# A transformer block of four samples on one core: the token shift, norm and feed-forward part of a layer done by halves of the tokens

## The chip, the cores and the metric

One core of a Trainium2 chip. The engines are PE (TensorE; PEld is its weight load), DVE (VectorE), ACT (ScalarE), POOL (GpSimd) and SP (SyncE, which here only issues DMAs). Each runs its own list of instructions in order and waits on semaphores. The metric is the device time of one execution in microseconds.

## What is computed

Four samples of 512 tokens x 128 channels, all in float32. Each goes through a first cross attention, then two layers of the kind below, then a second attention block, and a mixture of experts. Only the layer matters here:

```
def _layer(x, wqkv, qs, ksc, wo, lg, lb, w1, b1, w2, b2):
    ...                                    # local attention over windows of 64, 8 heads of 64
    x = x + o @ wo
    h = shift_token(x)                     # second half of the channels: from the token before
    mu = h.mean(-1, keepdims=True)
    var = h.var(-1, keepdims=True)
    h = (h - mu) / jnp.sqrt(var + 1e-05) * lg + lb
    h = h @ w1 + b1                        # 128 -> 2 x 341
    a, g = jnp.split(h, 2, axis=-1)
    h = a * jax.nn.gelu(g, approximate=False)
    x = x + h @ w2 + b2                    # 341 -> 128
    return x
```

## The kernel before

The 512 tokens of a sample lie as `TILES` = 4 tiles of `P` = 128 partitions. There are two slots of buffers (u = 0 and 1); slot 0 takes samples 0 and then 2, slot 1 takes 1 and then 3. For each engine a generator `sample_steps` yields once a step, and `in_turn` runs the generators of the two slots in turn after the list `TURNS`: slot 0 is ten steps ahead, and from there on one step of slot 0 alternates with one of slot 1. A third stream, `deferred_experts`, puts the experts of samples 0 and 1 between the steps of samples 2 and 3, chunk by chunk. So the order on each engine is fixed when the program is built, and step k of slot 0 stands beside step k-10 of slot 1.

A layer has 23 steps. Step 0 transposes y into `hTs`. Steps 1 to 8 project q, k and v of the four tiles (L438, L443 on PE), rotate q and k (`rotate`, L1141 and L1145 on DVE; `add_partners`, L1549 on POOL), transpose q (`turn_q`, L450) and k (`turn_k`, L457), sum squares (L1152) and compute inverse norms (`inverse_norms`, L1159 to L1164, in steps 4 and 8), by which POOL then scales k (`normalise_k`, L1555). Steps 9 and 10 make the first scores (L469 on PE, `take_scores`, L1122 on DVE). Steps 11 to 15 are the attention loop: exponentials (L855 on ACT), division (L1509 on POOL), transposes, mixing with the values (L499), output projection (L509) and, on DVE, `add_attention` (L1195), which adds tiles 0 to 3 to y in steps 13 to 16.

What stands behind that is here called the tail of the layer. In step 16 SP waits for the last tile of y and issues four DMAs that write `shifted` (L1714, L1716 twice, L1717). In step 18 DVE takes the norm's statistics (L1091, L1094), POOL computes `rstd` with an add and a power (L1491, L1492), in step 19 DVE applies it (L1100). In step 20 PE transposes the four tiles (L425) and ACT copies them with gain and bias (L840). In step 21 PE expands (three chunks, each a gate product, L705, into one of the 3 `act_psum` banks and a value product, L708, into one of the 4 `dve_psum` banks), ACT applies Gelu (L1012), DVE adds the bias and multiplies (L1378). In step 22 PE contracts (L715) and DVE adds the residual (L1383), which POOL had made in step 17 (L1495). There are 8 tails, counted here in order of time by the start of their shift: tail 1 (sample 0, layer 0) at 96.6 us, tail 2 (sample 1, layer 0) at 147.0, tail 3 at 203.0, tail 4 (sample 1, layer 1) at 254.5, tail 5 at 482.7, tail 6 at 543.2, tail 7 at 609.7 and tail 8 at 670.0 us; 5 to 8 are those of samples 2 and 3. Steps 17 to 19 hold nothing for PE and ACT.

ACT must have the table of the function it applies: Exp, Gelu and the experts' Silu need different ones, and the compiler puts a load of 1283 ns where the function changes (in the rows of the chain an entry `ACT L...` without a tile's name is such a load). A wait on a semaphore stands on an engine's list like an instruction, so all that is behind it waits too.

## Time and profile before

| | |
|---|---|
| time, median of 3 | 886.76 us (885.13 to 886.98) |
| the profiled execution | 885.65 us, of which its span 883.9 us |
| busy: PE, DVE, ACT, POOL | 82%, 64%, 60%, 34% of the span |
| granted TensorE clock | 0.902 of 2.4 GHz on average |
| table loads on ACT | 56, of 1283 ns each |

A row of the timeline gives the start in us, the duration, engine and line, the output and inputs, and in brackets how long the engine stood idle before it and what ended that. The chain of work that ended last is followed back from the last instruction; its rows give the start, the time on the chain and the work. The rows that are used stand below the change.

### The profile page before, as it was taken

Reading aid. Unit: us, or ns where it says so; the run is one execution under the profiler, and the core shown is the slowest. Engines: PE = TensorE matmul, PEld = TensorE weight load, DVE = VectorE, ACT = ScalarE, POOL = GpSimd, SP = SyncE. Lnnn points to the kernel's source line nnn. Section 1 sums busy time; section 2 is a strip of 40 time slices with the busy share of each in tenths; the row PEclk is TensorE's granted clock in tenths of the full one; section 3 lists DMA queues with packets and bytes.
Section 4 is the critical chain, followed back from the end, with each engine's and each line's share of the span. In section 5 each row is a group of like instructions: output and inputs, shape, how many; then the busy total and the mean of one; then the engine's idle time right before and its main releaser. Section 6 shows DMA issues by size and latency. Waiting matters only on the chain.

```text
span 883.9 us, 15786 instructions
## 1 busy us (share of the span) xinstructions
PE 723.4 (82%) x5368; PEld 472.7 (53%) x5368; DVE 569.2 (64%) x2212; ACT 533.9 (60%) x1345; POOL 304.5 (34%) x296
## 2 busy tenths in 40 slices
PE   5758788897878775788869789869887898889997
PEld 3436465564556654554546465546564664675443
DVE  5676856778657748648867757647566575873623
ACT  3348495775827336355596695795785845544442
POOL 4254524455421233223445324335233124312200
PEclk9888999998987978789999999999899898879999
DMA  8610010101100000202121301200202001004252
GB/s 260 193 29 15 14 43 13 39 6 22 34 13 1 2 1 1 82 2 68 36 67 37 90 14 45 75 1 22 69 26 56 18 26 30 13 13 125 73 129 91
DMA packets 37162, 41.83 MB, mean 47 GB/s; under 512 B 14345, under 2 KB 23771, under 8 KB 36955
## 3 DMA queue, kind: packets, MB, share of 16 engines
q1 hardware_dynamic: 37083, 40.83, 16.8%
q8 instruction: 43, 0.70, 0.3%
q14 instruction: 36, 0.29, 0.1%
HBM read 28.75 MB, written 2.62 MB: 35 GB/s over the span
## 4 chain that ended last, share of the span: by engine, by line
PE 45%; DVE 26%; ACT 17%; POOL 6%; issue 3%; DMA 1%; SPq 1%; DVEq 0%; POOLq 0%; ACTq 0%
ACT work L855 8%; PE act_psum L606 5%; PE moe_psum L616 5%; PE dve_psum L438 4%; PE act_psum L499 3%; PE dve_psum L509 3%; DVE work L1122 3%; DVE stats L1091 2%; DVE res_nrm L1100 2%; PE act_psum L705 2%; PE act_psum L768 2%; PE dve_psum L708 2%; PE dve_psum L715 2%; POOL work L1509 2%; PE act_psum L425 2%
## 5 line engine op out<-in xcount | busy, mean ns | idle before, releaser
L1509 POOL TENSOR_TENSOR work<-work,rinv 128x512 f32<-128x512 f32 (+1 forms) x72 | 77.6, 1085 | 147.2 <-DVE rinv L1108 146.8
L855 ACT ACTIVATE work<-work,nbias,rnorm 128x128 f32<-128x128 f32 x256 | 122.6, 481 | 7.9 <-DVE nbias L1185 7.5
L1491 POOL TENSOR_SCALAR rstd<-mv 128x4 f32<-128x4 f32 x36 | 10.0, 277 | 173.0 <-DVE mv L1094 172.8
L1549 POOL TENSOR_TENSOR hT<-hT,work 128x512 f32<-128x512 f32 x32 | 40.7, 1271 | 77.9 <-DVE work L1145 77.9
L438 PE MATMUL dve_psum<-wqkv,hTs 128*128 128x512 f32 x128 | 66.0, 640 | 1.5 <-ACT hTs L1002 1.3
L838 ACT COPY v_loc<-act_psum 77x512 f32<-77x512 f32 (+2 forms) x72 | 41.5, 582 | 36.0 <-PE act_psum L443 16.6
L1122 DVE CUSTOM_DVE_ANT_0 work<-dve_psum,masks 128x128 f32<-128x128 f32 x256 | 58.3, 282 | 3.3 <-PE dve_psum L469 3.3
L425 PE MATMUL act_psum<-ident,res_nrm 128*128 128x128 f32 x96 | 25.3, 363 | 41.9 <-DVE res_nrm L1100 41.9
L838 ACT COPY hT<-act_psum 128x512 f32<-128x512 f32 (+1 forms) x60 | 31.1, 523 | 43.7 <-PE act_psum L499 22.4
L953 ACT ACTIVATE work<-act_psum,cols 128x512 f32<-128x512 f32 x40 | 27.4, 687 | 36.3 <-PE act_psum L606 36.2
L1555 POOL TENSOR_TENSOR v_loc<-v_loc,rnorm 128x512 f32<-128x512 f32 x32 | 33.3, 1062 | 46.0 <-DVE rnorm L1164 46.0
L1141 DVE TENSOR_TENSOR hT<-dve_psum,tab_a 128x512 f32<-128x512 f32 x32 | 22.1, 690 | 41.8 <-PE act_psum L450 25.6
L1108 DVE RECIPROCAL rinv<-sums 128x4 f32<-128x4 f32 x96 | 14.4, 167 | 52.5 <-ACT work L855 52.5
L855 ACT ACTIVATION_READ_ACCUMULATOR work<-work,nbias,rnorm 128x1 f32 x256 | 48.0, 188 | 0.0
L840 ACT ACTIVATE hT<-act_psum,cols 128x512 f32<-128x512 f32 x16 | 12.4, 775 | 54.9 <-PE act_psum L425 54.9
L425 PEld LDWEIGHTS act_psum<-ident,res_nrm 128*128 128x128 f32 x96 | 14.9, 162 | 55.0 <-issue 34.7
L1145 DVE TENSOR_TENSOR work<-dve_psum,tab_b 128x512 f32<-128x512 f32 x64 | 43.6, 681 | 0.0
L1549 POOL TENSOR_TENSOR v_loc<-v_loc,work 128x512 f32<-128x512 f32 x32 | 42.0, 1313 | 0.4 <-DVE work L1145 0.4
L479 PE MATMUL dve_psum<-ident,work 128*128 128x128 f32 x128 | 21.0, 289 | 25.7 <-POOL work L1509 22.3
L469 PE MATMUL dve_psum<-kT,qT 64*64 64x128 f32 x1024 | 40.9, 306 | 0.8 <-ACT units L969 0.4
L1492 POOL TENSOR_TENSOR rstd<-rstd,neg_half 128x4 f32<-128x4 f32 x36 | 38.4, 1065 | 3.0
L855 ACT ACTIVATE work<-work,nbias 128x154 f32<-128x154 f32 x64 | 26.2, 410 | 21.3 <-DVE nbias L1238 21.3
(224 smaller groups left out, 2015.3 us busy)
## 6 DMA issues: line engine op xcount, KB each, us to landing
ahead<-cwT_dram SPq DMA_DIRECT2D x128, 64.0 KB, 2.0
v_loc<-v_loc SPq DMA_DIRECT2D x24, 256.0 KB, 3.7
kT<-cwT_dram SPq DMA_DIRECT2D x80, 64.0 KB, 2.1
qT<-cwT_dram SPq DMA_DIRECT2D x48, 64.0 KB, 2.0
wqkv<-in_wqkv_dram SPq DMA_DIRECT2D x2, 768.0 KB
res_nrm<-in_x_dram SPq DMA_DIRECT2D x4, 256.0 KB, 3.1
w_m<-in_w_m_dram SPq DMA_DIRECT2D x1, 1024.0 KB, 8.7
v_loc<-v_loc SPq DMA_DIRECT2D x8, 128.0 KB, 3.2
```

The lines of the kernel that those rows point to most:

```text
L425: last = nc.tensor.transpose(bank[:, t * P:(t + 1) * P], src[u][:, t, :], ident[:])
L438: nc.tensor.matmul(bank[:], h, attn_w[:, k * INNER:(k + 1) * INNER], start=True, stop=True)\
L469: last = nc.tensor.matmul(banks[odd][half * WINDOW:(half + 1) * WINDOW, c * KEYS:(c + 1) * KEYS], qT[u][d, c, at:at + WINDOW], kT[u][d, c, ...
L606: nc.tensor.matmul(bank[:], w, given[:], start=True, stop=True).then_inc(act_filled, 1)
L616: nc.tensor.matmul(moe_psum[:], w, units_of, start=(c == 0), stop=False)
L838: nc.scalar.copy(dst, bank[0:n, 0:w]).then_inc(act_emptied, 1)
L855: last = nc.scalar.activation(weights[:, i, :], weights[:, i, :], ACT.Exp, bias=nbias[u][:, b, i:i + 1], scale=scale_of(i), accum_out=sums ...
L1122: return nc.vector.tensor_tensor_reduce(out=weights, in0=bank[:, at:at + width], in1=mask, scale=1.0, scalar=LOWEST, op0=ALU.add, op1=ALU. ...
L1145: nc.vector.tensor_tensor(partners[u][:, t % 2, k, :].rearrange(halves, s=2, d=DH // 2), bank[:].rearrange(halves, s=2, d=DH // 2)[:, :, : ...
L1492: nc.gpsimd.tensor_tensor(rstd[u][:], rstd[u][:], neg_half[:, 0:TILES], ALU.pow).then_inc(ln_rstd[u], 1)
L1509: nc.gpsimd.tensor_tensor(some, some, by.unsqueeze(2).to_broadcast(list(some.shape)), ALU.mult).then_inc(ready[u], 1)
L1549: nc.gpsimd.tensor_tensor(own, own, partners[u][:, t % 2, k, :], ALU.add).then_inc(turned_ready[u], 1)
```

## The change

The tail is done in two halves of two tiles each. The token shift of tiles 0 and 1 is issued in step 14, as soon as `add_attention` has added tile 1; its statistics are taken in step 15, `rstd` by POOL in step 15, and it is applied in step 16. PE transposes that half in step 17, expands it in step 18 and contracts it in step 19; the second half follows the old places: shift in step 16, statistics in 18, applied in 19, transposed in 20, expanded in 21, contracted in 22. The number of steps is the same. `shifted` has two places, one for each half, and two semaphores. Gelu, the product with the gate, the copy behind the transposes and the residual add are each split into two of 256 columns, and so are the two products of the expansion; the transposes and the contraction's matmuls are as many as before. The four shift DMAs become two sets of four, each half as large, and the `rstd` pair on POOL is issued twice on half as many elements. ACT has 68 table loads where it had 56. Line numbers of the changed kernel are higher by 8 (PE, L425 to L509 there L433 to L517), 21 (ACT) and 30 to 35 (DVE).

```diff
-LN_XATTN, LN_OUTER, LN_FF, LN_TGT, LN_1, LN_2, LN_3, LN_MOE = 0, 1, (2, 3), 4, 5, 6, 7, 8
+LN_XATTN, LN_OUTER, LN_FF, LN_TGT, LN_1, LN_2, LN_3, LN_MOE = 0, 1, ((2, 3), (4, 5)), 6, 7, 8, 9, 10
+PAIR = TILES // 2
+HALVES = ((0, PAIR), (PAIR, TILES))
...
-shifted = [v[:, 2 * TILES - 1, :].rearrange("p (t d) -> p t d", t=TILES) for v in v_loc]
+shifted = [[v[:, tile, 0:PAIR * D].rearrange("p (t d) -> p t d", t=PAIR) for tile in (TILES + 1, 2 * TILES - 1)] for v in v_loc]
...
                 yield from local_attention_steps(l, u)
-                yield
-                yield
-                yield
-                transpose_norm(("hT_ff", l, u), LN_FF[l], u)
-                yield
-                pe.wait_ge(act_emptied, act_item["hT_ff", l, u] + 1)
-                for m, w in enumerate(HID_W):
-                    bank = act_bank(("ff_g", l, m, u))
-                    nc.tensor.matmul(bank[0:w, :], w1[:, l, HID + m * P:HID + m * P + w], hT[u][:],
-                                     start=True, stop=True).then_inc(act_filled, 1)
-                    bank = dve_bank(("ff_a", l, m, u))
-                    nc.tensor.matmul(bank[0:w, :], w1[:, l, m * P:m * P + w], hT[u][:],
-                                     start=True, stop=True).then_inc(dve_filled, 1)
-                yield
-                pe.wait_ge(dve_emptied, dve_item["ff_a", l, len(HID_W) - 1, u] + 1)
-                bank = dve_bank(("ff_out", l, u))
-                for t in range(TILES):
+                def turn_half(g):
+                    transpose_tiles(("hT_ff", l, u, g), nrm, u, LN_FF[l][g], *HALVES[g])
...
+                def expand_half(g):
+                    tokens = slice(HALVES[g][0] * P, HALVES[g][1] * P)
+                    pe.wait_ge(act_emptied, act_item["hT_ff", l, u, g] + 1)
...
+                def contract_half(g):
+                    pe.wait_ge(dve_emptied, dve_item["ff_a", l, len(HID_W) - 1, u, g] + 1)
+                    bank = dve_bank(("ff_out", l, u, g))
...
+                    last.then_inc(dve_filled, 1)
+
+                turn_half(0)
+                yield
+                expand_half(0)
+                yield
+                contract_half(0)
+                yield
+                turn_half(1)
+                yield
+                expand_half(1)
+                yield
+                contract_half(1)
                 yield
...
                 yield from local_attention_steps(l, u)
-                yield
-                yield
-                yield
-                copy_bank(("hT_ff", l, u), hT[u][:], bias=col("ln_b", l), scale=col("ln_g", l))
-                yield
-                for m, w in enumerate(HID_W):
-                    bank = filled(("ff_g", l, m, u))
-                    nc.scalar.activation(gel[u][0:w, m, :], bank[0:w, :], ACT.Gelu, bias=col("b1g", 3 * l + m, w))\
-                      .then_inc(act_emptied, 1)
-                yield
-                yield
+                for g in range(2):
+                    tokens = slice(HALVES[g][0] * P, HALVES[g][1] * P)
+                    copy_bank(("hT_ff", l, u, g), hT[u][:, tokens], bias=col("ln_b", l), scale=col("ln_g", l), w=PAIR * P)
+                    yield
+                    for m, w in enumerate(HID_W):
+                        bank = filled(("ff_g", l, m, u, g))
+                        nc.scalar.activation(gel[u][0:w, m, tokens], bank[0:w, 0:PAIR * P], ACT.Gelu, bias=col("b1g", 3 * l + m, w))\
+                          .then_inc(act_emptied, 1)
+                    yield
+                    yield
...
+        def shifted_stats(l, u, g):
+            dve.wait_ge((shift_early, shift_late)[g][u], 4 * 16 * (l + 1))
+            for i, t in enumerate(range(*HALVES[g])):
...
+        def shifted_apply(l, u, g):
+            dve.wait_ge(ln_rstd[u], LN_FF[l][g] + 1)
+            for i, t in enumerate(range(*HALVES[g])):
...
@@ -1215,13 +1250,17 @@
                     take_pt_lo(n, u)
                 if n >= 2:
                     add_attention(n - 2, u)
+                if n == PAIR + 1:
+                    link(nc.vector.memset(shifted[u][0][0:1, 0, D // 2:D], 0.0))
+                if n == TILES:
+                    shifted_stats(l, u, 0)
                 if n + 1 < TILES:
                     invert_sums(u, sm_local(l, n + 1), (n + 1) % 2)
                 if n + 2 < TILES:
                     take_scores(n + 2, u)
                 yield
             add_attention(TILES - 1, u)
-            link(nc.vector.memset(shifted[u][0:1, 0, D // 2:D], 0.0))
+            shifted_apply(l, u, 0)
...
                 yield from local_attention_steps(l, u)
-                yield
-                dve.wait_ge(shift_done[u], 4 * 16 * (l + 1))
-                norm_stats(shifted, u)
-                yield
-                norm_apply(LN_FF[l], shifted, nrm, u)
-                yield
-                yield
-                for m, w in enumerate(HID_W):
-                    bank = filled(("ff_a", l, m, u))
...
-                bank = filled(("ff_out", l, u))
-                dve.wait_ge(res_ready[u], l + 1)
-                nc.vector.tensor_tensor(flat(y[u]), bank[:], flat(res[u]), ALU.add).then_inc(dve_emptied, 1)
+                def gate_half(g):
+                    tokens = slice(HALVES[g][0] * P, HALVES[g][1] * P)
...
+                def add_half(g):
+                    bank = filled(("ff_out", l, u, g))
...
+                                            ALU.add).then_inc(dve_emptied, 1)
+
+                yield
+                shifted_stats(l, u, 1)
+                gate_half(0)
+                yield
+                shifted_apply(l, u, 1)
+                add_half(0)
+                yield
+                yield
+                gate_half(1)
+                yield
+                add_half(1)
                 if l == LAYERS - 1:
...
                 yield
+                norm_rstd(LN_FF[l][0], u, *HALVES[0])
                 yield
                 yield
...
                 yield
-                norm_rstd(LN_FF[l], u)
+                norm_rstd(LN_FF[l][1], u, *HALVES[1])
                 yield
...
-                for _ in range(1 + TILES + 1):
+                def shift_half(g, done):
+
+                    first, end = HALVES[g]
+                    sp.wait_ge(dve_emptied, dve_item["attn_out", l, end - 1, u] + 1)
+                    for lo, hi in ((0, 112), (112, P - 1)):
+                        sp.dma_start(shifted[u][g][lo + 1:hi + 1, :, half:D], y[u][lo:hi, first:end, half:D]).then_inc(done[u], 16)
+                    start = max(first, 1)
+                    sp.dma_start(shifted[u][g][0:1, start - first:, half:D], y[u][P - 1:P, start - 1:end - 1, half:D]).then_inc(done[u], 16)
+                    sp.dma_start(shifted[u][g][:, :, 0:half], y[u][:, first:end, 0:half]).then_inc(done[u], 16)
+
+                for _ in range(1 + PAIR + 1):
                     yield
-                sp.wait_ge(dve_emptied, dve_item["attn_out", l, TILES - 1, u] + 1)
-                sp.dma_start(shifted[u][:, :, 0:half], y[u][:, :, 0:half]).then_inc(shift_done[u], 16)
-                for lo, hi in ((0, 112), (112, P - 1)):
-                    sp.dma_start(shifted[u][lo + 1:hi + 1, :, half:D], y[u][lo:hi, :, half:D]).then_inc(shift_done[u], 16)
-                sp.dma_start(shifted[u][0:1, 1:TILES, half:D], y[u][P - 1:P, 0:TILES - 1, half:D])\
-                  .then_inc(shift_done[u], 16)
+                shift_half(0, shift_early)
+                yield
+                yield
+                shift_half(1, shift_late)
                 yield
```

On PE in tail 1, behind the output projection of tile 3 (dve_psum3 <- wo). Of before:

```order
L509 MATMUL dve_psum3<-wo,hT0 128x128 x4
L443 MATMUL act_psum0<-wqkv,hTs1 128x512
L457 MATMUL act_psum1<-ident,v_loc1 128x128 x4
L438 MATMUL dve_psum0<-wqkv,hTs1 128x512
L438 MATMUL dve_psum1<-wqkv,hTs1 128x512
L450 MATMUL act_psum2<-ident,hT1 128x128 x4
L457 MATMUL act_psum0<-ident,v_loc1 128x128 x4
L443 MATMUL act_psum1<-wqkv,hTs1 128x512
```

and of after:

```order
L517 MATMUL dve_psum3<-wo,hT0 128x128 x4
L451 MATMUL act_psum0<-wqkv,hTs1 128x512
L465 MATMUL act_psum1<-ident,v_loc1 128x128 x4
L433 MATMUL act_psum2<-ident,res_nrm0 128x128 x2
L446 MATMUL dve_psum0<-wqkv,hTs1 128x512
L446 MATMUL dve_psum1<-wqkv,hTs1 128x512
L458 MATMUL act_psum0<-ident,hT1 128x128 x4
L465 MATMUL act_psum1<-ident,v_loc1 128x128 x4
L713 MATMUL act_psum2<-hT0,w1 128x256
L716 MATMUL dve_psum2<-hT0,w1 128x256
...
L451 MATMUL act_psum2<-wqkv,hTs1 128x512
L724 MATMUL dve_psum1<-w2,qT0 128x128 x6
```

The first half's transposes now stand ahead of slot 1's q and k projection (L446), and its expansion and contraction behind that.

On DVE in the same place, from the add of tile 2 on (y0 <- dve_psum0). Of before:

```order
L1195 TENSOR_TENSOR y0<-dve_psum0,y0 128x128
L1141 TENSOR_TENSOR hT1<-dve_psum1,tab_a 128x512
...
L1195 TENSOR_TENSOR y0<-dve_psum3,y0 128x128
L1224 MEMSET v_loc0 1x64
L1152 TENSOR_REDUCE sumsq1<-res_nrm1 128x16
L1141 TENSOR_TENSOR hT1<-dve_psum0,tab_a 128x512
...
L1091 BN_STATS stats0<-v_loc0 128x6 x4
L1094 BN_AGGR mv0<-stats0 128x2 x4
L1152 TENSOR_REDUCE sumsq1<-work1 128x16
...
L1100 TENSOR_SCALAR res_nrm0<-v_loc0,mv0,rstd0 128x128 x4
```

and of after:

```order
L1230 TENSOR_TENSOR y0<-dve_psum0,y0 128x128
L1126 BN_STATS stats0<-v_loc0 128x6 x2
...
L1230 TENSOR_TENSOR y0<-dve_psum3,y0 128x128
L1135 TENSOR_SCALAR res_nrm0<-v_loc0,mv0,rstd0 128x128 x2
L1187 TENSOR_REDUCE sumsq1<-res_nrm1 128x16
L1176 TENSOR_TENSOR hT1<-dve_psum0,tab_a 128x512
...
L1412 SCALAR_TENSOR_TENSOR qT0<-dve_psum2,cols,work0 128x256
L1412 SCALAR_TENSOR_TENSOR qT0<-dve_psum3,cols,work0 128x256
L1412 SCALAR_TENSOR_TENSOR qT0<-dve_psum0,cols,work0 85x256
L1187 TENSOR_REDUCE sumsq1<-work1 128x16
...
L1420 TENSOR_TENSOR y0<-dve_psum1,res_nrm0 128x256
```

Statistics and application of the first half moved ahead of slot 1's sums and rotations, and the first half's gating (L1412) came in ahead of slot 1's last sum of squares and inverse norms.

On ACT in tail 5, between the copies of the two halves (hT0 <- act_psum). Of before:

```order
L969 ACTIVATE units0<-act_psum2,cols 128x512
L838 COPY v_loc1<-act_psum0 128x512
L969 ACTIVATE units1<-act_psum1,cols 128x512
L879 COPY qT1<-act_psum2 128x4x128
L840 ACTIVATE hT0<-act_psum0,cols 128x512
L855 ACT_TABLE_LOAD
```

and of after:

```order
L990 ACTIVATE units0<-act_psum1,cols 128x512
L1032 ACT_TABLE_LOAD
L1032 ACTIVATE work0<-act_psum2,cols 128x256
...
L859 COPY v_loc1<-act_psum2 128x512
L990 ACT_TABLE_LOAD
L990 ACTIVATE units1<-act_psum0,cols 128x512
L900 COPY qT1<-act_psum1 128x4x128
L861 ACTIVATE hT0<-act_psum2,cols 128x256
L876 ACT_TABLE_LOAD
```

Two table loads and the three half Gelus came in ahead of slot 1's exponentials (L876), where one Silu had followed the other. Behind them the order of loads is the old one.

## Rows read from the trace of the kernel before

**Rows 1.** The page's chain that ended last: shares of the span by engine.
```profile
PE 45%; DVE 26%; ACT 17%; POOL 6%; issue 3%; DMA 1%; SPq 1%; DVEq 0%; POOLq 0%; ACTq 0%
```
**Rows 2.** Stretches: length; busy us of PE, PEld, DVE, ACT, POOL; PE clock; DMA.
```profile
96.00:112.00 16.00, 9.86 (x94) 6.60 (x93) 14.48 (x60) 7.29 (x20) 8.83 (x9) 0.85 0.09 18
112.00:128.00 16.00, 14.75 (x154) 10.17 (x153) 7.75 (x38) 14.26 (x43) 4.75 (x5) 0.94 0.24 59
...
254.00:270.00 16.00, 10.29 (x45) 6.21 (x46) 9.64 (x61) 6.67 (x23) 7.09 (x8) 0.61 0.09 18
...
482.00:498.00 16.00, 12.51 (x90) 7.23 (x92) 15.02 (x43) 7.08 (x13) 9.79 (x9) 0.95 0.19 50
498.00:518.00 20.00, 18.36 (x170) 12.10 (x166) 10.38 (x58) 19.85 (x46) 4.53 (x4) 0.96 0.28 74
```
**Rows 3.** Waits of PE (total, times, longest): tail 1 (80:128), tail 8 (670:706).
```profile
PE act_psum L425 <- DVE res_nrm L1100: 4.7, 3, 3.5
...
PE act_psum L705 <- ACT hT L840: 4.2, 1, 4.2
```
**Rows 4.** Timeline of tail 1: start, duration, instruction, idle time before it.
```profile
88.70 0.28 DVE L1195 TENSOR_TENSOR y<-dve_psum,y 128x128 f32<-128x128 f32 x1
...
92.49 0.28 DVE L1195 TENSOR_TENSOR y<-dve_psum,y 128x128 f32<-128x128 f32 x1
...
95.92 1.88 PE L438 MATMUL dve_psum<-wqkv,hTs 128*128 128x512 f32 x4
...
96.33 0.28 DVE L1195 TENSOR_TENSOR y<-dve_psum,y 128x128 f32<-128x128 f32 x1
...
98.27 0.69 DVE L1141 TENSOR_TENSOR hT<-dve_psum,tab_a 128x512 f32<-128x512 f32 x1 [0.35 <-PE act_psum L450]
...
105.62 2.61 DVE L1100 TENSOR_SCALAR res_nrm<-v_loc,mv,rstd 128x128 f32<-128x128 f32 x4
...
106.11 0.30 PE L425 MATMUL act_psum<-ident,res_nrm 128*128 128x128 f32 x1 [3.46 <-DVE res_nrm L1100]
...
109.48 0.48 ACT L855 ACTIVATE work<-work,nbias,rnorm 128x128 f32<-128x128 f32 x1
```
**Rows 5.** Chain that ended last, tail 1: start, duration, what.
```profile
99.11 1.72 DMA v_loc<-y
...
124.99 3.93 ACT work L855 x16
```
**Rows 6.** Timeline of tail 2: adds of tiles 1 and 2, and slot 0's rotation.
```profile
139.60 0.28 DVE L1195 TENSOR_TENSOR y<-dve_psum,y 128x128 f32<-128x128 f32 x1
...
140.92 0.28 DVE L1195 TENSOR_TENSOR y<-dve_psum,y 128x128 f32<-128x128 f32 x1
...
144.33 0.69 DVE L1141 TENSOR_TENSOR hT<-dve_psum,tab_a 128x512 f32<-128x512 f32 x1 [3.13 <-PE act_psum L450]
```
**Rows 7.** Chain that ended last, tail 2 (one expansion pair, one contraction).
```profile
161.50 0.86 PE dve_psum L708 x2
...
167.26 2.90 PE dve_psum L715 x24
```
**Rows 8.** Chain that ended last, tail 4.
```profile
258.21 3.80 PE act_psum L759 x4
```
**Rows 9.** Chain that ended last, tail 5, on ACT.
```profile
505.38 0.69 ACT units L969
506.08 1.28 ACT L1012
507.38 1.83 ACT work L1012 x3
```
**Rows 10.** Groups by line and shape: count, busy us, mean ns of one.
```profile
L1012 ACT ACTIVATE work<-act_psum,cols 128x512 f32<-128x512 f32 x16 | 10.4, 685 | 0.6 <-PE act_psum L705 0.4
...
L840 ACT ACTIVATE kcT<-act_psum,cols 128x154 f32<-128x154 f32 x4 | 1.6, 391 | 1.3 <-PE act_psum L651 1.3
...
L1378 DVE SCALAR_TENSOR_TENSOR qT<-dve_psum,cols,work 128x512 f32<-128x512 f32 x16 | 11.4, 747 | 24.9 <-ACT work L1012 24.6 <-issue 0.2
...
L1492 POOL TENSOR_TENSOR rstd<-rstd,neg_half 128x4 f32<-128x4 f32 x36 | 38.4, 1065 | 3.0
```

62 lines of the change are left out of this document (43 added, 19 removed).

## The prediction

> **What bounds the kernel now.** I read the page's chain first: PE has 45% of it, DVE 26%, ACT 17% [rows 1], so no engine bounds the whole, and each stretch must be read by itself. The stretches around the tails [rows 2] come next. Ahead of the transposes of tail 1 (96 to 112 us) DVE is busy 14.48 of 16 us and PE 9.86; behind them (112 to 128) PE has 14.75 and ACT 14.26 of 16. In tail 5 it is the same with experts between: DVE 15.02 of 16 ahead, then ACT 19.85 of 20. So the front of such a tail goes by DVE and its rear by ACT and PE. The waits say where PE stands: 4.7 us in tail 1 at the transposes (L425), 4.2 at the expansion (L705) in tail 8 [rows 3]. These two kinds of wait, read for all eight tails, are 4.7, 1.8, 4.5, 5.4, 5.1, 1.9, 3.8 and 6.3 us, 33.5 in all (the first and the last have their rows in [rows 3]). The timeline [rows 4] shows why in tail 1: the add of tile 3 is at 96.33, the shift lands at 100.83 [rows 5], but DVE applies the norm only at 105.62, since slot 1's rotation, last sum of squares and inverse norms stand between. PE waits 3.46 us for it.
>
> **What is moved, in work.** Half a tail on PE is half the contraction, 2.90/2 = 1.45, half the expansion, 3 x 0.86 = 2.58 [rows 7], and half the transposes, about 0.2: 4.2 us. It goes from a rear to a front in which PE waits. On ACT, 512 columns take 685 ns and 154 with the same kind of operands 391 [rows 10], 0.82 ns a column; a chained Gelu takes 1.83/3 = 0.61 us [rows 9], so a chained half is 0.61 - 0.21 = 0.40, three are 1.2. The rear loses 0.6 us of Gelu and 0.2 of the copy. On DVE a gate is 747 ns [rows 10]; the add of 128 columns takes 0.28 [rows 4], so a half lies between 0.37 and 0.51, three of them about 1.3 us. All halves together cost about 0.6 us more on DVE and 1.2 on ACT per tail than the wholes, and this overhead lies in the front.
>
> **Tail 1 (and 3), step by step.** The add of tile 1 ends at 88.98 [rows 4]. Four DMAs before took from the add (96.61) to the landing (100.83) 4.2 us [rows 4, 5]. I take the same for each set of halves, since most of it is issue; bounds 2.1 (half the size, half the time) and 4.2. Landing is then at 93.2, after the add of tile 2 (92.49 to 92.77), so DVE waits 0.4 us and takes statistics until 93.9. The rotation behind it had itself waited for PE, so that is free; the cover gone, it costs 0.4 + 0.65. Then the add of tile 3 and the first application, 0.7 to 1.3 us (four took 2.61 beside POOL work [rows 4]). **Here the change adds a wait**: PE's transposes of the first half wait for that application, and slot 1's q and k projection, which had begun at 95.92, ahead of DVE's add at 96.33, is queued behind. It begins near 98.3, takes 1.88, the transposes of q 0.44, so slot 1's rotation starts at about 100.6 in place of 98.27: 2.3 us late. It is followed by the second statistics (0.65 for 1.3) and the gating of the first half. That waits for the Gelus: copy, squares and q and k copies, a table load and three halves put their end near 104.5, so the gates end at 105.0. Behind the gates on DVE are queued slot 1's sum of squares and inverse norms (3.5 us), and behind those POOL's scaling of k. Then the second application (1.2 for 2.6) and the first residual add (0.4): slot 1's scores start at about 110.2 where they started at 108.15. The front is 2 us longer.
> In the rear, ACT must now load the Exp table behind the second copy, so exponentials start at about 112.5 for 109.48 [rows 4], 3.0 late. PE, which had 14.75 us of work there and ran at the lower of its two clocks (0.85 on average over the 96 to 112 stretch [rows 2]), has 4.2 us less and stands in nobody's way. ACT then runs without its waits: 3.9 exponentials, 1.05 copies, load, 1.2 Gelu, load, 3.9, 0.5, which puts the third tile's exponentials at 125.7 with every wait kept, 125.0 without the 0.7 us of waits at the first load. Before it was 124.99 [rows 5]. I take **0**, bounds +2 and -2 (gain positive from here on).
>
> **Tails 2 and 6.** The adds of tiles 1 and 2 lie only 1.3 us apart in tail 2 [rows 6], so the early statistics wait some 2.9 us for the DMA; DVE stood idle there for 3.13 us anyway [rows 6], so about 0.4 is left, and 0.65 of statistics and 0.75 of application stand ahead of inverse norms on the path. Front: 1.3 us longer in tail 2, 0.9 in tail 6. The `rstd` pair on POOL (1065 ns for the power [rows 10]; for two elements I take the same, bounds 0.5 and 1.1) falls into POOL's idle time in both. Rear: PE has 4.2 less, but DVE's chain rotation, sums, gates, scores is close behind, and gains only 0.75 of gates and 0.3 of the add, plus 0.3 of the application. **-0.3 and +0.4**; bounds -1.5 and, were PE the only bound, +3.
>
> **Tails 5 and 7.** The front is DVE's (15.02 of 16 [rows 2]); PE's 12.51 with 4.2 more would be 16.7, so PE gets as full as DVE. The q and k projection is late by 0.4 to 1. Front: 0.3 longer. Table loads: before, ACT loaded Exp, Silu, Gelu and Exp in the rear (one of them stands in [rows 9]), and it still does; the two more are in the front, where ACT had 7.08 of 16. The rear, ACT's with 19.85 of 20, is shorter by 0.8 and by 0.2 since the copy comes earlier than the load needs. **+0.7 each**, bounds -1.5 and +2.
>
> **Tails 4 and 8.** The clock was 0.61 from 254 to 270 us [rows 2], and the four matmuls at L759 took 3.80 us [rows 8]; at 0.43 each, as in [rows 7], they are 1.72. The first expansion comes ahead of them. At the low clock it takes up to 5.1, at the high one 2.6; the work that PE has no longer to wait for brings the clock back sooner, so I take 4.6 for it and 1.7 for L759, and slot 0's exponentials start 1 us late in tail 4, 3 in tail 8, where experts' products stand in the same queue. In the rear the expansion of 5 to 8 us at low clock becomes half of it at a clock that has mostly returned, and the contraction's 2.9 us [rows 7] becomes half. **+2.5 and +1.0**; bounds -2 and +5 each.
>
> **The sum.** 0 + 0 - 0.3 + 0.4 + 0.7 + 0.7 + 2.5 + 1.0 = 5.0 us. The profiled execution was 885.65 us (883.9 of span and 1.75 around it), so 880.65; the median of the runs lies 1.1 higher, so **881.7**.
>
> **The rivals.** (a) PE's waits turn into work nearly one for one. For: 33.5 us of waits, and the shift is up to 8 us earlier. With at most 4.2 a tail they give 28.5; against it stands that DVE is nearly full in front of six of the tails, so half, 14 us: 873. Chance 0.17. (b) **Slower: PE stands at the early transposes and holds slot 1's projection back.** Place: step 17 of each tail. Price: 2.3 in tails 1 and 3, 1.3 in 2 and 6, 1.0 in 5 and 7, and in 4 and 8, where the expansion stands ahead of the q projection, 2.3 each: 13.8 us, against 6 us that the rears still give: 894. It decides when the gates of the first half end more than about 1 us later than I have them, since then DVE's chain is late by that in every tail. Chance 0.17. (c) The table loads come out on the path. ACT goes from 56 loads to 68, 12 x 1.28 = 15.4 us [rows 9]. On the path altogether they turn the gain of 5 into a loss of 10: 897. For: in tail 1 one of them stands between the second copy and the exponentials; against: 8 of the 12 lie in fronts where ACT was half idle. Chance 0.08. (d) The change does not do what it says: the first half runs where it should, but every stretch is as long as before, because DVE sets the front and ACT the rear. 886.8, chance 0.10.
> A load's own time is 1.28 us, and in tail 5 nothing else is lost around it: the Silu ahead of it ends at 506.07, the load runs from 506.08 to 507.36, the Gelus start at 507.38 [rows 9]. The Trainium skill (ScalarE: Activation LUTs, "What ACT_TABLE_LOAD costs") adds a drain of about 1.38 us to each and gives 2.66 us for a switch; by it the twelve would take 32 us, and (c) would end near 914. The trace does not agree, and its rule to batch activations by set, which speaks against this change, weighs here what [rows 9] give.
>
> **How the numbers follow.** Forecast 0.48; its own range is 876 to 887. Of it nine tenths lie more than 0.2% (1.8 us, about what a measurement here can tell) below 886.76. Faster: 0.43 + 0.17 = 0.60. Within 0.2%: 0.05 + 0.10 = 0.15. Slower: 0.17 + 0.08 = 0.25. The range reaches to (a) and (b), 871 to 893, and leaves (c) and the far ends of (a) and (b) out.
>
> **What would show it.** Right: PE's wait at L425 in tails 1, 3, 5 and 7 largely gone at the second half; a new one of 1 to 2 us at the first half; slot 1's rotation in step 7 later by about 2 us; the first gates waiting for Gelu; exponentials after tail 5 starting as early as before and ending 0.8 us sooner; the clock in tail 4 above 0.61; 68 loads of 1283 ns. Wrong: if PE's new waits at the first half are over 3 us, (b); if ACT is busy right up to the exponentials in the fronts, (c); if the shift of a half lands in much under 4.2 us, the fronts are shorter than worked out and (a) gains.

## The result: 895.5 us, slower by 1.2%

The changed kernel takes 895.49 us (median of 4 runs, 893.60 to 897.73); the kernel before, beside it, takes 885.94 (884.08 to 886.98). The ratio is 1.0117 (95% interval 1.0092 to 1.0141). The forecast was 881.7 with a range of 871 to 893: sign and range were both missed. The profiled execution of the changed kernel took 893.60 us, its span 891.8.

First the page of the changed kernel: busy time of the engines, then the shares of the chain that ended last.

```profile
PE 727.8 (82%) x5464; PEld 492.4 (55%) x5464; DVE 580.5 (65%) x2244; ACT 556.7 (62%) x1389; POOL 309.7 (35%) x312
...
PE 39%; DVE 29%; ACT 21%; POOL 4%; issue 4%; DMA 1%; SPq 1%; DVEq 0%; POOLq 0%; ACTq 0%
```

Against [rows 1] PE has lost 6 points of the chain, DVE has won 3 and ACT 4. The chain has moved off the engine that has most of the work onto two that hand work to each other. ACT is busy 22.8 us more than before (533.9), 15.4 of it in 12 more table loads (68 for 56), DVE 11.3 more (569.2), PE 4.4 (723.4).

Where the time went is best read from marks that both kernels have. Between the last add of attention in a tail and the exponentials of the other slot's last tile lies the tail; from there to the next last add lies the way to the next tail. The differences to the kernel before, in us, worked out from the start times in the two timelines:

| | 1 | 2 | 3 | 4 | 5 | 6 | 7 | 8 |
|---|---|---|---|---|---|---|---|---|
| changed: tail | +5.9 | 0.0 | +1.3 | -1.8 | +0.7 | +0.5 | +0.9 | +1.4 |
| changed: way to the next | +0.7 | +1.4 | 0.0 | +0.9 | +1.0 | -1.3 | +0.3 | -3.2 |

(In 4 and 8 the mark behind the tail is the second set of the cross attention's exponentials; the way behind 8 is the rest of the kernel. Ahead of tail 1 it was 0.9 us early.) Nearly six of the eight microseconds are in tail 1. Such a trace is one execution, and where it stands at the last add ahead of tail 1 scatters: slot1 below reached it 3.7 us earlier than the kernel before, with the same instructions up to there. Distances between marks are the safer reading.

The timeline of tail 1 in the changed kernel, with start, duration, instruction and the idle time before it:

```profile
92.33 0.48 DVE L1126 BATCH_NORM_STATS2 stats<-v_loc 128x6 f32<-128x128 f32 x2 [1.13 <-DMA v_loc<-y]
...
95.43 0.28 DVE L1230 TENSOR_TENSOR y<-dve_psum,y 128x128 f32<-128x128 f32 x1
95.62 1.26 POOL L1600 TENSOR_TENSOR v_loc<-v_loc,work 128x512 f32<-128x512 f32 x1
95.63 2.56 DVE L1135 TENSOR_SCALAR res_nrm<-v_loc,mv,rstd 128x128 f32<-128x128 f32 x2
...
96.84 1.26 POOL L1546 TENSOR_TENSOR res_nrm<-y,rows 128x512 f32<-128x512 f32 x1
97.11 0.38 PE L433 MATMUL act_psum<-ident,res_nrm 128*128 128x128 f32 x1 [2.80 <-DVE res_nrm L1135]
...
98.24 0.47 PE L433 MATMUL act_psum<-ident,res_nrm 128*128 128x128 f32 x1 [0.75 <-DVE res_nrm L1135]
```

PE stands 2.80 and 0.75 us for two applications of the norm, which take 2.56 us and end (98.19) as GpSimd's work does (98.10). What comes of it is in the chain that ended last (start, duration, what):

```profile
98.71 3.41 PE dve_psum L446 x4
102.13 0.85 PE act_psum L458 x4
...
104.47 1.28 ACT L1032
...
107.15 0.47 DVE qT L1412
107.62 1.14 DVE sumsq L1187
...
112.54 0.35 PE act_psum L433
112.89 0.02 issue
112.91 0.56 ACT hT L861
113.47 0.02 issue
113.49 1.28 ACT L876
114.77 0.01 issue
114.79 3.92 ACT work L876 x16
```

Slot 1's q and k projection (L446), 1.88 us at 95.92 in [rows 4], starts at 98.50 and takes 3.62 from its start to its end. Rotation, table load, Gelu, gates and only then slot 1's sum of squares follow, and behind the second half's copy one more load. The exponentials begin at 114.79; in [rows 4] they began at 109.48. From the last add to these exponentials it was 13.2 us and is 19.4. Of the 6.2 more, 3.5 lie ahead of the projection (it began 0.41 us before the add and now begins 3.08 behind it), 2.1 between its start and slot 1's first rotation (4.51 us for 2.36, the low level of the clock), and 0.6 behind that.

The stretches of the same kernel (length; busy us of PE, PEld, DVE, ACT, POOL; PE clock; DMA):

```profile
96.00:104.00 8.00, 6.14 (x15) 3.69 (x16) 4.29 (x5) 2.47 (x5) 2.10 (x2) 0.57 0.09 17
...
254.00:270.00 16.00, 12.74 (x100) 10.27 (x95) 9.76 (x45) 6.00 (x10) 6.54 (x9) 0.89 0.08 17
```

The clock granted to PE is 0.57 in the first 8 us of tail 1, nearly all at 1.2 GHz, where PE had stood. In tail 4 it rose from 0.61 [rows 2] to 0.89.

In tail 3 the same instructions met GpSimd's bias add a little later. The two applications took 1.54 us, the projection began 1.96 us behind the add, and it ran at the high level:

```profile
209.96 1.54 DVE L1135 TENSOR_SCALAR res_nrm<-v_loc,mv,rstd 128x128 f32<-128x128 f32 x2
...
211.72 1.88 PE L446 MATMUL dve_psum<-wqkv,hTs 128*128 128x512 f32 x4
```

There the way from the add to the exponentials grew by 2.7 us (13.1 to 15.8) and not by 6.2.

### The profile page after: what moved, and what is told of

Same layout as the page of the kernel before. It is cut to its first block, busy times and chain, and to the rows that moved or that the text cites. A ratio compares the mean times of both kernels' runs of the same rounds, so it can differ in the third digit from the quotient of the medians.

```text
span 891.8 us, 16160 instructions
## 1 busy us (share of the span) xinstructions
PE 727.8 (82%) x5464; PEld 492.4 (55%) x5464; DVE 580.5 (65%) x2244; ACT 556.7 (62%) x1389; POOL 309.7 (35%) x312
## 4 chain that ended last, share of the span: by engine, by line
PE 39%; DVE 29%; ACT 21%; POOL 4%; issue 4%; DMA 1%; SPq 1%; DVEq 0%; POOLq 0%; ACTq 0%
ACT work L876 10%; PE dve_psum L446 5%; PE act_psum L614 5%; PE moe_psum L624 5%; DVE work L1180 3%; DVE work L1157 3%; PE act_psum L507 3%; ACT v_loc L876 2%; PE act_psum L789 2%; DVE stats L1111 2%; PE dve_psum L517 2%; DVE res_nrm L1135 2%; ACT L876 2%; PE dve_psum L796 2%; POOL work L1560 2%
## 5 line engine op out<-in xcount | busy, mean ns | idle before, releaser
L876 ACT ACTIVATE work<-work,nbias,rnorm 128x128 f32<-128x128 f32 x256 | 122.7, 481 | 13.1 <-DVE nbias L1220 12.8
L1542 POOL TENSOR_SCALAR rstd<-mv 128x4 f32<-128x4 f32 (+1 forms) x44 | 11.7, 266 | 175.6 <-DVE mv L1114 148.5
L446 PE MATMUL dve_psum<-wqkv,hTs 128*128 128x512 f32 x128 | 68.5, 661 | 2.7 <-ACT hTs L1023 2.4
L433 PE MATMUL act_psum<-ident,res_nrm 128*128 128x128 f32 x96 | 24.6, 346 | 36.1 <-DVE res_nrm L1120 19.5
L713 PE MATMUL act_psum<-hT,w 128*128 128x256 f32 (+1 forms) x96 | 36.4, 467 | 16.4 <-ACT kT L892 10.6
L876 ACT ACTIVATION_READ_ACCUMULATOR work<-work,nbias,rnorm 128x1 f32 x256 | 48.0, 188 | 0.0
L1543 POOL TENSOR_TENSOR rstd<-rstd,neg_half 128x4 f32<-128x4 f32 (+1 forms) x44 | 42.5, 967 | 3.7
L861 ACT ACTIVATE hT<-act_psum,cols 128x256 f32<-128x256 f32 (+1 forms) x24 | 15.3, 636 | 44.8 <-PE act_psum L433 44.8
L433 PEld LDWEIGHTS act_psum<-ident,res_nrm 128*128 128x128 f32 x96 | 14.3, 155 | 50.6 <-issue 24.0
```

Source lines behind the costliest of these rows:

```text
L433: last = nc.tensor.transpose(bank[:, i * P:(i + 1) * P], src[u][:, t, :], ident[:])
L446: nc.tensor.matmul(bank[:], h, attn_w[:, k * INNER:(k + 1) * INNER], start=True, stop=True)\
L876: last = nc.scalar.activation(weights[:, i, :], weights[:, i, :], ACT.Exp, bias=nbias[u][:, b, i:i + 1], scale=scale_of(i), accum_out=sums ...
L1543: nc.gpsimd.tensor_tensor(some, some, neg_half[:, first:end], ALU.pow).then_inc(ln_rstd[u], 1)
```

## The experiments

All start from the changed kernel. In these kernels the tail's steps are read from tables (step: what is done, with 0 for the first half and 1 for the second), and a condition says which tails go by halves; with the tables and the condition as they stand in the changed kernel, its instructions and their order are the same. u is the sample (0 and 2 run in slot 0), l the layer. Ratios are against the kernel before, run beside each, with 95% intervals. Lines of TensorE stand 27 further down than in the changed kernel (transposes L460, projection L473, scores L504), those of VectorE and GpSimd some 40 (application L1173).

**Is it the place on PE, the gates, the loads, or the norm?**

```diff
 turn_late
-PE_TAIL = {17: ['turn0'], 18: ['expand0'], 19: ['contract0'], 20: ['turn1'], 21: ['expand1'], 22: ['contract1']}
-DVE_TAIL = {18: ['stats1', 'gate0'], 19: ['apply1', 'add0'], 21: ['gate1'], 22: ['add1']}
+PE_TAIL = {18: ['turn0'], 19: ['expand0'], 20: ['contract0', 'turn1'], 21: ['expand1'], 22: ['contract1']}
+DVE_TAIL = {18: ['stats1'], 19: ['apply1', 'gate0'], 20: ['add0'], 21: ['gate1'], 22: ['add1']}
```

> All of the first half's work behind its application comes one step later on every engine: transposes in step 18 (behind slot 1's q and k projection of its step 7 instead of ahead of it), expansion and gates in 19, contraction and add in 20, ahead of the second half's transposes. Statistics, factors and application stay where the changed kernel has them. Theory O (order on TensorE: the projection of slot 1 stands behind transposes that wait for the application, and then runs at the 1.2 GHz level, 3.41 us instead of 1.91 in the first tail): 4 to 5 us come back in each of the four tails of slot 0 where the other slot is in its first steps, less what hits the later expansion, so 886 to 889 us. Theory L (the twelve more table loads on ScalarE): no change, 895 us. Theory D (VectorE stands for the landing of the half set and for the first half's Gelu ahead of slot 1's norms): about 893, since the gates move but the statistics don't.

Measured: 895.17 us, ratio 1.0136 (1.0089 to 1.0182). Nothing came back. The projection did (1.88 us, from 93.43), and slot 1's last sum of squares was hardly late any more (it starts 6.9 us behind the last add, 5.7 before and 12.1 in the changed kernel). But another wait took the place of the one removed. The waits of PE in tail 1 (total, times, longest), then the chain that ended last:

```profile
PE dve_psum L504 <- DVE qT L1456: 5.1, 1, 5.1
```
```profile
107.47 1.99 PE dve_psum L504 x32
109.45 2.61 PE dve_psum L753 x12
...
112.32 0.57 ACT hT L884
112.90 1.28 ACT L899
114.20 1.93 ACT work L899 x7
```

Slot 1's first scores (L504) need two of the four banks that VectorE empties, and these are taken in turn: the three of the first half's expansion come first and are empty only when gated. So PE waits 5.1 us for a gate of the other slot, then contracts, then transposes; from the last add of tile 3 to the first exponentials it is 19.1 us, against 13.2 before and 19.4 in the changed kernel.

```diff
 gate_late
+PE_TAIL = {17: ['turn0'], 18: ['expand0'], 20: ['contract0', 'turn1'], 21: ['expand1'], 22: ['contract1']}
+DVE_TAIL = {18: ['stats1'], 19: ['apply1', 'gate0'], 20: ['add0'], 21: ['gate1'], 22: ['add1']}
```

> The first half's gates on VectorE move from step 18 to step 19, behind the second half's application and behind slot 1's inverse norms of its step 8; its contraction and add move to step 20, ahead of the second half's transposes. Transposes and expansion stay in 17 and 18. Theory D in its part on the gates (in the first tail sums of squares of slot 1 start at 107.54 behind gates that end 107.62, and these waited for a table load and a Gelu): 1 to 1.5 us back in each of the tails 1, 3, 5, 7, so 890 to 892. Theories O and L: within 1 us of the changed kernel, 894 to 896.

Measured: 903.66 us, ratio 1.0226 (1.0184 to 1.0268), 12 us over what was expected. It pays for both: the projection stands behind the early transposes as in the changed kernel (3.15 us behind the add, 3.17 us long, partly at the low level), and the scores wait 4.0 us for the gates. From add to exponentials it is 21.7 us. The theory that the gates merely stood in the wrong place on VectorE falls.

```diff
 no_gelu0
-    ACT.Gelu
+    ACT.Gelu if g == 1 else ACT.Identity
```

> The changed kernel with the first half's Gelu replaced by Identity, which needs no table of its own: the values of the first two tiles are then not the reference's, the work is the same except that the eight pairs of table loads of the first halves fall away or partly so (12 fewer loads are expected, 56 in all). Theory L: of the loads that the chain of waits shows in the changed kernel 6 more stand than before (26 against 20), so 6 to 9 us come back: 886 to 889. Theory O: the projection's wait and its clock are untouched, so no more than the single load in front of the first gates, 1.3 us in one or two tails: 893 to 895.

Measured: 893.35 us, ratio 1.0099 (1.0063 to 1.0135), with 56 loads. About 2 us came back where the theory of the loads gave 6 to 9, and the intervals don't exclude none. So the loads alone don't explain it.

```diff
 norm_only
-def ff_split(l, u): return True
+def ff_split(l, u): return False
```

(The norm's halves have a condition of their own and stay; where this one is false, everything from the transposes to the add is whole, in steps 20 to 22. Where only norm_split is shown changed below, ff_split follows it.)

> Only token shift and norm go by halves, at the changed kernel's places; transposes, Hidden copy, expansion, Gelu, gates, contraction and add are whole and stand where the kernel before has them (steps 20 to 22). 56 table loads. Theories O and L alike: the loss is in the feed-forward part of the first half, so the time is that of the kernel before or a little under it, 885 to 887. Theory D in its part on the landing (idle time of VectorE before the shifted statistics until the transfer has landed is 10.8 us in 7 places against 3.1 in 2 before): the loss of these waits stays, 889 to 892.

Measured: 881.30 us, ratio 0.9965 (0.9941 to 0.9989), faster than before. The loss is in the feed-forward halves, 13 us of them, and the early norm is a gain.

**Which tails, and what kind of cost?**

```diff
 slot1, tails_13, norm_ff_last
-def norm_split(l, u): return True
+def norm_split(l, u): return u % 2 == 1                      # slot1
+def norm_split(l, u): return u == 0                          # tails_13
+def ff_split(l, u): return u % 2 == 1 and l == LAYERS - 1    # norm_ff_last, norm_split true in all
```

> The whole change in the tails of slot 1 alone (2, 4, 6, 8); in those of slot 0 (1, 3, 5, 7) shift, norm and feed-forward part are whole and stand where the kernel before has them. By now: moving only the order on TensorE or only the gates gave nothing back, and norms alone by halves made the kernel faster; so the loss is made by the first half's feed-forward work where slot 1 is in its first steps (its gates wait for Gelu on VectorE ahead of slot 1's norms, or, moved behind them, hold the four banks that VectorE reads and with them slot 1's first scores). Theory R (that place: the odd tails): the loss is gone, 884 to 888. Theory H (the halves' own work, 5.5% more instructions everywhere): half of the loss stays, about 890.

Measured: 883.90 us, ratio 0.9980 (0.9960 to 0.9999). The loss is gone: it is in slot 0's tails.

> The whole change in the tails 1 and 3 alone (the first sample's two layers); the other six as in the kernel before. The marks in the traces put 5.9 us and 1.4 us of the changed kernel's loss into these two, and 0.9 to 3 us each into tails 5 and 7. If the marks hold: 885.6 + 7 to 9, so 891 to 895, and slot 1's first exponentials in tail 1 start 6 us later after the last add than before. If the loss is spread evenly over the odd tails (11 us over four): 890 to 892. If the marks mislead: under 888.

Measured: 892.85 us, ratio 1.0099 (1.0073 to 1.0126): two tails carry nearly the whole loss. In this trace the other six are as before (marks within 1.1 us); tail 1 costs 5.8, the way into tail 3 3.4 and tail 3 itself 3.9. The chain that ended last of tails_13 around tail 3:

```profile
200.11 0.66 SPq L1810
...
200.81 0.94 SPq L1810
...
201.79 1.43 SPq L1812
...
203.27 2.05 DMA v_loc<-y
...
206.66 0.68 DVE work L1218
...
208.73 2.48 DVE res_nrm L1173 x2
...
211.59 3.41 PE dve_psum L473 x4
```

VectorE stands 1.28 us for the landing of the half set, which takes 5.2 us from issue to landing, with slot 1's rotation and slot 0's adds queued behind; then two applications take 2.48 and the projection 3.41, as in tail 1.

> Shift and norm by halves in all eight tails, the feed-forward part by halves in the tails 4 and 8 alone, where slot 0 is behind its own tail and does the second attention's steps. In the changed kernel the time from the last add of tail 4 to the marks behind it was about 1.6 us shorter than before, in tail 8 about 1.7. So 2 to 4 us under norm_only. If the gain of these two tails came from the norm alone, no difference from norm_only.

Measured: 881.79 us, ratio 0.9958 (0.9939 to 0.9978). No difference from norm_only, where 2 to 4 us less were expected: feed-forward halves gain nothing even in tails 4 and 8.

```diff
 ff_behind
+PE_TAIL = {19: ['turn0'], 20: ['expand0', 'turn1'], 21: ['contract0', 'expand1'], 22: ['contract1']}
+DVE_TAIL = {18: ['stats1'], 19: ['apply1'], 20: ['gate0'], 21: ['add0', 'gate1'], 22: ['add1']}
 behind_flat: also ACT.Gelu if g == 1 else ACT.Identity
 ff_same, from norm_lag
+PE_TAIL = {20: ['turn0', 'turn1'], 21: ['expand0', 'expand1'], 22: ['contract0', 'contract1']}
+DVE_TAIL = {18: ['stats1'], 19: ['apply1'], 21: ['gate0', 'gate1'], 22: ['add0', 'add1']}
```

> Halves everywhere as in the changed kernel, but the first half's feed-forward part stands behind slot 1's norms and beside its first scores: transposes in step 19, expansion and gates in 20, contraction and add in 21, each one step ahead of the second half's. Work and instruction counts are those of the changed kernel; only the place differs. Theory R (the place): near norm_only and the kernel before, 882 to 888. Theory H (the halves' own work and their table loads, 12 more): 892 to 896.

> norm_lag with every feed-forward step by halves but in place: both halves' transposes and copies in step 20, both expansions, Gelus and gates in 21, both contractions and adds in 22. So 56 table loads as in norm_lag, nothing moved, and only the halves' own work added: 5464 matmuls in the changed kernel against 5240-odd in the whole ones, twice as many turns of the three banks that ScalarE reads and of the four that VectorE reads. norm_lag takes 879.7, ff_behind (halves one step apart, 12 loads more) 893.9. Theory H (fixed work of halves and the banks' turns): most of these 14 us are here too, 888 to 893. Theory M (it is the move: what stands between the halves' steps and the loads): 880 to 884.

> ff_behind (first half's transposes in step 19, expansion and gates in 20, contraction in 21, everything by halves) with Identity in place of the first halves' Gelu, so the values of those tiles are not the reference's; the table loads go back towards 56. ff_behind's ratio is 1.0098, the one of the halves in place 0.9975. Theory L (behind slot 1's norms, where ScalarE goes from one tile's exponentials to the next, each pair of loads is on the path: 8 x 1.28 or more): most of the 11 us come back, ratio 0.997 to 1.002. Theory R (banks and queues: the expansion ahead of slot 1's second scores): ratio stays over 1.006.

Measured: ff_behind 893.88 us, ratio 1.0098 (1.0065 to 1.0131); ff_same 881.41, 0.9975 (0.9956 to 0.9994); behind_flat 887.07, 1.0021 (0.9997 to 1.0046). My theory of the place gave ff_behind 882 to 888 and was wrong. The halves' own work is small: ff_same has twice as many expansions, Gelus and gates as norm_lag (below) and is 4 us over it by the ratios. One step apart, the halves cost 11 us more, and 6.8 of these (3 to 10, by both intervals) are table loads: ff_behind has 30 of them on its chain, behind_flat 22, ff_same 23. They stand right ahead of exponentials. The chain that ended last of ff_behind in tail 1:

```profile
109.76 0.56 ACT hT L884
...
110.34 1.28 ACT L899
...
111.64 0.49 ACT work L899
```

The remaining 4 us between behind_flat and ff_same stay open; they differ in the step of the early statistics too.

**What tails 1 and 3 are made of.**

```diff
 bias_13 (in tails 1 and 3), bias_late (in all eight), on GpSimd
-add_bias(u, row("b2", l))
-yield
-norm_rstd(LN_FF[l][1], u, *HALVES[1])
+yield
+norm_rstd(LN_FF[l][1], u, *HALVES[1])
+add_bias(u, row("b2", l))
 warm_13, on TensorE, in the bank taken for the first half's transposes
+for _ in range(6):
+    nc.tensor.matmul(bank[:], ident[:], wqkv[:, 0, 0:INNER], start=True, stop=True)
 loads_13: tails_13 with ACT.Gelu if g == 1 else ACT.Identity; both_13: bias_13 and loads_13
```

> The changed kernel with one edit: GpSimd adds the bias to the residual (512 columns, 1.27 us) a step later, behind the factors of the second half instead of ahead of them. Theory P (the port: VectorE's application of the norm stands while GpSimd works; two applications took 2.56 us in the first tail and end at 98.19, with GpSimd's work ending at 98.10, where two alone take 0.56): the first application in tails 1, 5 and 7 is 1.2 us shorter, slot 1's projection starts 1.2 us earlier, and 1 to 4 us come back in all: 891 to 894. Without such an effect: 895 plus or minus 1.

> tails_13 with GpSimd's bias add of these two tails behind the factors of the second half. Theory P (port): two applications took 2.5 us in both tails, and one of the two pieces of GpSimd's work beside them is this add; they take 1.3 instead, slot 1's projection begins 1.2 us earlier in both: 1.5 to 3 us back, 890 to 891.5. No such effect: 892.9.

> tails_13 (the whole change in tails 1 and 3, the others whole) with six matmuls of 512 columns (0.43 us each at 2.4 GHz, 2.6 us) that nothing reads, ahead of the first half's transposes, in the bank which these overwrite. They fit into the wait for the first application (2.8 us idle in the first tail). Theory C (the clock: four matmuls of slot 1's q and k projection took 3.41 us at 1.2 GHz in both tails where they take 1.91 or less): these matmuls take 1.9 us or less again, what follows is earlier by 1.5 to 2 in each of the two tails, 3 to 4 us back: 888.5 to 890 beside 885.6 of before. If the wait alone counts: 892.5 or somewhat more.

> tails_13 with Identity in place of Gelu in the first half of these two tails (the values of two tiles are not the reference's); 56 table loads instead of 60. The chain of tails_13 shows two or three loads in each tail where before it shows none; one of them, ahead of the first half's Gelu, and one ahead of the first exponentials fall away. Theory L: 2 x 2.6 less, 888. Theory O (order, port and clock): the load ahead of the Gelu is 1.3 us in front of the gates and of slot 1's norms, the other again 1.3 ahead of the exponentials behind them, but PE and the clock are untouched: 1 to 3 us back, 890 to 892.

> The change in tails 1 and 3 alone, with both edits at once: the bias add behind the second factors (bias_13, 1.0100 alone) and Identity in place of the first half's Gelu (loads_13, 1.0086 alone); tails_13 has 1.0099. In the traces each edit shortened the way from the last add of tail 1 to slot 1's first exponentials from 19.3 us to 18.2, against 13.2 before. If the causes lie one behind the other, both together give 2 x 1.1 in each tail, ratio 1.005 to 1.007. If they cover for one another: 1.008 to 1.010. In both cases what stays of the way, 17 us for 13, is the wait of TensorE for the application with the 1.2 GHz level behind it.

| | us | ratio | 95% interval | projection, tail 1 | add to exponentials, tail 1 | tail 1 to tail 4, over before |
|---|---|---|---|---|---|---|
| before | | | | 1.88 | 13.2 | |
| changed | 895.49 | 1.0117 | 1.0092 to 1.0141 | 3.62 | 19.4 | +9.4 |
| bias_late | 891.14 | 1.0075 | 1.0055 to 1.0096 | 2.86 | 17.7 | +7.4 |
| tails_13 | 892.85 | 1.0099 | 1.0073 to 1.0126 | 3.62 | 19.3 | +11.9 |
| bias_13 | 893.10 | 1.0100 | 1.0073 to 1.0126 | 3.47 | 18.2 | +9.0 |
| warm_13 | 895.28 | 1.0124 | 1.0088 to 1.0160 | 1.88 | 17.8 | +7.8 |
| loads_13 | 892.71 | 1.0086 | 1.0059 to 1.0114 | 3.62 | 18.2 | +8.9 |
| both_13 | 890.17 | 1.0074 | 1.0041 to 1.0108 | 1.88 | 15.4 | +3.7 |

(The last column runs from the last add of tail 1 to that of tail 4.)

The times can't tell tails_13 and the four edits of it apart well, since each edit is worth less than their intervals. The traces can. Add to exponentials falls from 19.3 by 1.1 us with the bias add out of the way (two applications took 1.59 us, not 2.5, and the projection begins 2.1 us behind the add and not 3.1), by 1.1 with one load out of the way, and by 1.5 with the projection at the high level. both_13 has the first two, and in tail 1 its projection ran at the high level too, which its expectation had not foreseen; its 3.9 is about the sum of the three (3.7). So the causes lie one behind the other. What is left of it, 2.2 us over before, is the projection's later start: 1.96 us behind the add, where before it began 0.41 ahead of it. In tail 3 of both_13 the clock was low again (3.35 us) and the way 17.0. From tail 1 to tail 4, bias add and load are worth 2.9 and 3.0 us and both together 8.2. (both_13 leaves the first half's Gelu out as loads_13 does.) The times of bias_13 and warm_13 did not follow, and that of both_13 (1.0074) lies between what the two theories gave, so the sum is shown by one trace of each. Why bias_late gained in time what bias_13 did not stays open.

warm_13 says less than it was meant to, for a reason of its own. The chain that ended last of warm_13 (transposes and fill L458, projection L475), then the stretch:

```profile
95.00 5.15 PE act_psum L458 x12
...
100.37 1.72 PE dve_psum L475 x4
```
```profile
95.00:100.00 5.00, 5.00 (x13) 2.08 (x13) 5.00 (x7) 0.67 (x2) 3.73 (x4) 1.00 0.07 15
```

The filling was put at 2.6 us and took 5.15, at the high level (granted clock 1.00): each of the six float32 matmuls of 512 columns is two instructions on PE, of 0.43 us each. So it kept the clock up, but it also kept PE until 100.15, and the projection began 4.0 us behind the add where it had begun 3.1 behind it. The high level gave back 2.1 us up to the rotation, the filling took 0.9 of them. From tail 1 to tail 4 this trace is 4.1 us shorter than that of tails_13; it then loses 3.8 us over before on the way to tail 5, where its instructions are those of before and tails_13 is 0.9 under it. Why, and why the times show no gain, stays open. A filling of half the size was not run.

**What the gain of the norm rests on.**

```diff
 norm_lag: norm_only, but (with the first half's factors on GpSimd a step later too)
-    step 15: shifted_stats(l, u, 0)     step 16: shifted_apply(l, u, 0)
+    step 16: shifted_stats(l, u, 0)     step 17: shifted_apply(l, u, 0)
 lag_bias: norm_lag with the bias add as in bias_late
 lag_turn: norm_lag, but
+PE_TAIL = {19: ['turn0'], 20: ['turn1'], 21: ['expand1'], 22: ['contract1']}
+ACT_TAIL = {19: ['copy0'], 20: ['copy1'], 21: ['gelu1']}
```

In lag_turn turn and copy go two tiles and two; expand1, gelu1 and contract1 are the whole ones.

> As norm_only (shift and norm by halves, the feed-forward part whole and at its old places), but the first half's statistics and factors a step later (step 16, behind the add of the last tile) and its application in step 17. The shift stays in step 14. Theory D-landing (statistics at step 15 stand for the landing of the half set; VectorE waited 10.8 us in 7 places in the changed kernel against 3.1 in 2 before, and adds of the third tail came 1.8 us further apart in norm_only): 1 us back in four or more tails, 2 to 4 us under norm_only's time. If these waits are covered anyway: within 1 us of norm_only.

> norm_lag with the bias add a step later, as in bias_late. Theory P: the early applications (1.5 us for two, with GpSimd beside them) get shorter, but no engine stands for them there, so 879.7 or up to 1.5 us less. If the bias add in its new place hits the second application or the scaling of k: up to 2 us more.

> norm_lag with the transposes and the Hidden copy by halves too, the first half's in step 19, ahead of slot 1's first scores; expansion and all behind it whole, 56 loads. In step 20 half of the transposes and of the copy (0.6 us) are then left. Expected: 0 to 1.5 us under norm_lag (879.7), and if transposes ahead of slot 1's scores do harm wherever they stand: 1 to 2 over it.

Measured: norm_lag 879.66 us, ratio 0.9927 (0.9904 to 0.9950), 3.4 us under norm_only by the ratios, as the wait for the landing had it (the intervals overlap); lag_bias 881.32, 0.9967 (0.9952 to 0.9982), so the bias add is better where it was; lag_turn 875.48, 0.9893 (0.9860 to 0.9927), faster than both kernels, by 9 us and 20, and by the ratios 3 us under norm_lag, where at most 1.5 was expected; these two intervals overlap. It keeps what is short and needs no table by halves, behind slot 1's norms, and everything that takes banks of VectorE's or calls a table whole. Its marks stand 1.6 us better than before in tails 7 and 8, 1.2 in 5, 2.1 in 4 and 0.7 in 1 and 3. In tail 5, before (chain that ended last):

```profile
495.19 1.09 DVE res_nrm L1100
...
496.33 0.75 PE act_psum L425 x2
...
497.10 0.78 ACT hT L840
...
497.89 1.28 ACT L855
...
499.19 0.97 ACT work L855 x3
```

and in norm_lag at the same place:

```profile
494.43 0.33 DVE res_nrm L1173
...
495.45 1.54 DVE units L1381
...
497.87 0.17 DVE nbias L1258
...
498.07 1.93 ACT work L899 x7
```

The last application, the transposes, the copy and the load stood between slot 1's norms and its exponentials; with half of the set done earlier the load is off the path, and VectorE's expert work and scores set the start.

## Why the prediction was wrong

**Tails 1 and 3, taken at 0: the step that failed.** By the marks the eight tails lose about 9 us where 5.0 were to be gained; 7.2 of the loss are in these two. The mechanism was named: the projection of slot 1 is queued behind transposes that wait for the application. Two terms of that step were mis-sized. The first is the application, "0.7 to 1.3 us": it took 2.56, since it stood for two additions of GpSimd. The second is "It begins near 98.3, takes 1.88, the transposes of q 0.44". The projection took 3.62 and the transposes 0.85, because PE had stood for 2.8 us and worked at 1.2 GHz. I had read the clock of 0.85 in [rows 2] as a fact of the old stretch, not as something that the new wait would do to the work behind it; and the 14.75 us that the prediction puts beside it belong to the next stretch, at 0.94.

That the start came out (98.3 said, 98.50 measured) is luck: this trace was 1.8 us ahead at the add of tile 1, from which the prediction counts (87.21 for 88.98). Counted from there, the start was 2.0 us later than said, and slot 1's rotation 4.2 (15.8 us behind the add for 11.6). The landing was put at 4.2 us and took 5.1 (from 87.21, the end of the add, to 92.31), so VectorE stood 1.13 us, not 0.4. The gates were to end at 105.0 and ended at 107.62, the exponentials were to start at 112.5 and did at 114.79.

Tail 3 is the test of the rest. There the application took 1.54 us and the projection 1.88, and counted from the last add the rotation was 2.4 us later than before (2.3 said) and the exponentials 2.7 (3.0 said). So the path was right where those two terms came near.

The rear did not give back what was said. In tail 1 the third tile's exponentials start at 128.79 (125.0 to 125.7 said). Behind them PE, which had stood 1.65 and 1.25 us for GpSimd's division, worked at the low level again, where before it had the high one (1.08 us for the same 32 matmuls):

```profile
129.90 1.91 PE act_psum L507 x32
```

That is why the last tile's exponentials come 7.2 us later and not 6.0, at 136.01; before they were at 130.97. In tail 3, where the way to the first exponentials had grown by 2.7, the tail lost 1.3.

**Rival (b)** was that case, with a chance of 0.17, a time of 894 and the point from which it decides: gates more than 1 us later than worked out. They were 2.6 later, and PE's waits at the first half were 3.55 us, over the 3 that were to show it. Its price of 2.3 per tail was too low in tail 1 and too high elsewhere, and turn_late shows that its cure, a step later, doesn't work: the banks in turn make another wait of it. That coupling was in neither forecast nor rivals.

**Tails 5 and 7, +0.7 each:** -0.7 and -0.9. The front was to be 0.3 longer and is 2.7: from the last add to slot 1's norms it was 8.1 us (482.38 to 490.43) and is 10.7 (489.95 to 500.67). Behind the norms exponentials start 1.4 us sooner (7.4 for 8.8), more than the 0.8 said; that half of the argument held, and norm_lag shows it alone. **Tails 2 and 6, -0.3 and +0.4:** 0 and -0.5, within their bounds (the terms given for tail 2, 1.35 less 1.3, make about 0, not -0.3). **Tails 4 and 8, +2.5 and +1.0:** +1.8 and -1.4. The clock rose as said, and the q projection took 1.72 for 3.80, as said:

```profile
269.59 1.72 PE act_psum L780 x4
```

But lag_turn gets 2.1 us in tail 4 and 1.6 in tail 8 without feed-forward halves.

**Rival (c), the loads:** 12 more, as said, and 1.28 us each. Their share of the chain grew by 6 (26 for 20). They explain perhaps 2 us of the changed kernel, and 6.8 in ff_behind, where nothing else hid them. Of the halves' overhead, ACT's was right (22.8 less 15.4 leaves 7.4 for 9.6 said), DVE's not: 11.3 for 4.8. The group of the shifted norm's application says where, with count, busy us and mean ns:

```profile
L1135 DVE TENSOR_SCALAR res_nrm<-v_loc,mv,rstd 128x128 f32<-128x128 f32 x32 | 21.4, 711 | 2.8 <-POOL rstd L1543 2.8
```

The same 32 instructions took 14.9 us in the kernel before.

**Rival (a)** was right in one point: PE's waits for the second half did shrink, 1.5 us in tail 1 for the 4.7 of [rows 3]. With the new 3.55 at the first half the sum is 5.0. **Rival (d)**, no change, lies outside the interval.
